# Delta-rule recurrence with loads behind the update, and gates at the head of TensorE's step

## The reference, cut to what matters

```
def step(S, inp):
    qt, kt, vt, at, bt = inp
    err = jnp.einsum('bhij,bhj->bhi', S, kt) - vt
    S = at[..., None] * S - bt[..., None, None] * (err[..., None] * kt[:, :, None, :])
    o = jnp.einsum('bhij,bhj->bhi', S, qt)
    return (S, o)
```

## Time and profile before

| | us |
|---|---|
| median of 3 runs | 7999.06 |
| lowest, highest | 7984.93, 7999.54 |
| profiled execution | 7956.72 |
| its span | 7954.9 |
| VectorE busy | 5439.6 (68%) |
| TensorE busy | 5251.1 (66%) |
| GpSimd busy | 3640.6 (46%) |
| ScalarE (ACT) busy | 3251.7 (41%) |
| mean granted TensorE clock | 0.748 of 2.4 GHz |

### The profile page before, as it was taken

The page is one execution under the profiler, slowest core; times in us unless marked ns, Lnnn a source line. Parts: engine busy times, 40 slices in busy tenths (PEclk is TensorE's granted clock), DMA queues, the critical chain, the costliest instruction groups (busy, mean ns, idle before and its releaser), DMA issues. The chain is left out here.

```text
span 7954.9 us, 175685 instructions
## 1 busy us (share of the span) xinstructions
PE 5251.1 (66%) x58695; PEld 3467.7 (44%) x58695; DVE 5439.6 (68%) x16005; ACT 3251.7 (41%) x6914; POOL 3640.6 (46%) x4232
## 2 busy tenths in 40 slices
PE   5665656656565565655656653577777777777787
PEld 4444444444444444444444443333333333433333
DVE  5777777777877778777777775566656565565655
ACT  4434344343343434434434342244444444344444
POOL 3666676666766667666666666111111111111110
PEclk7766667666676666767767676688888888888888
DMA  4556565565655656556565564111111111121111
GB/s 108 131 133 141 123 144 131 133 141 123 144 128 135 140 122 147 128 134 142 125 143 129 133 144 110 51 44 40 43 40 43 40 40 47 51 50 41 43 40 33
DMA packets 1172906, 786.91 MB, mean 99 GB/s; under 512 B 1039923, under 2 KB 1091795, under 8 KB 1157844
## 3 DMA queue, kind: packets, MB, share of 16 engines
q1 hardware_dynamic: 864468, 583.96, 31.6%
q10 hardware_dynamic: 307712, 193.48, 10.1%
HBM read 473.80 MB, written 303.50 MB: 98 GB/s over the span
## 5 line engine op out<-in xcount | busy, mean ns | idle before, releaser
L588 PE MATMUL p_bank<-xnT,wqkv 128*128 128x128 f32 x4096 | 708.4, 348 | 571.7 <-ACT st L652 571.7
L461 POOL TENSOR_TENSOR qp<-qp,pt 128x512 f32<-128x512 f32 (+7 forms) x1024 | 965.8, 943 | 85.4 <-issue 5.2
L493 PE MATMUL d_bank<-xd,kt 32*64 32x128 f32 x7936 | 411.8, 363 | 881.4 <-issue 399.2
L456 POOL TENSOR_TENSOR qp<-qp,ab 128x512 f32<-128x512 f32 (+7 forms) x1024 | 906.9, 886 | 75.3
L588 PEld LDWEIGHTS p_bank<-xnT,wqkv 128*128 128x128 f32 x4096 | 669.8, 258 | 598.9 <-issue 598.9
L810 DVE SCALAR_TENSOR_TENSOR p_bank<-y,conv_w,p_bank 128x128 f32<-128x128 f32 x3072 | 828.5, 349 | 93.4 <-ACT p_bank L639 77.3
L1682 DVE TENSOR_REDUCE nmax<-w_bank 128x1 f32<-128x512 f32 x1024 | 638.2, 684 | 325.4 <-PE w_bank L1308 315.6
L1263 POOL TENSOR_TENSOR ot<-ot,ln_w 128x1024 f32<-128x1024 f32 x64 | 150.6, 2353 | 1424.2 <-ACT ot L1538 1424.2
L458 POOL TENSOR_TENSOR pt<-qp,vb 128x512 f32<-128x512 f32 (+7 forms) x1024 | 792.6, 774 | 9.3 <-DVE vb L887 9.3
L828 DVE TENSOR_TENSOR st<-d_bank,st 128x512 f32<-128x512 f32 x496 | 320.2, 687 | 674.0 <-PE d_bank L493 661.5
L493 PEld LDWEIGHTS d_bank<-xd,kt 32*64 32x64 f32 x7936 | 327.0, 182 | 940.3 <-issue 934.4
(11 more groups left out here) (219 smaller groups left out, 11569.3 us busy)
## 6 DMA issues: line engine op xcount, KB each, us to landing
decay_or_prod<-decay_dram SPq DMA_DIRECT2D x124, 1024.0 KB, 15.5
prod_dram<-decay_or_prod ACTq DMA_DIRECT2D x64, 1280.0 KB, 7.7
kp<-prod_dram SPq DMA_DIRECT2D x64, 640.0 KB, 6.9
qp<-prod_dram SPq DMA_DIRECT2D x64, 640.0 KB, 9.7
a_dram<-at ACTq DMA_DIRECT2D x64, 512.0 KB
ab<-a_dram SPq DMA_DIRECT2D x64, 512.0 KB, 5.9
v_dram<-vt ACTq DMA_DIRECT2D x64, 512.0 KB
vb<-v_dram SPq DMA_DIRECT2D x64, 512.0 KB, 3.9
```

The lines of the kernel that those rows point to most:

```text
L456: link(nc.gpsimd.tensor_tensor(q, q, ab[:, g, r:r + 1, :].to_broadcast([128, w, DV]), ALU.mult), 1)
L461: link(nc.gpsimd.tensor_tensor(q, q, pt2[:, 0:w], ALU.add))
L493: last[e] = nc.tensor.matmul(d_bank[e][64 * par:64 * par + 64, 128 * k:128 * k + 128], kt[32 * q:32 * q + 32, g, DK * h:DK * h + DK], xd[3 ...
L588: mm = nc.tensor.matmul(bank[:, 128 * i:128 * i + 128], wqkv[:, k, 128 * m:128 * m + 128], xnT[:, g, k, :], start=k == 0, stop=k == 1)
```

## The change

Four things are done.

1. SyncE issues the two spread loads of the decays for step s - 1 in slot s, behind the eight `xd` loads and ahead of `o_dram`, where before it issued them at the end of slot s - 1.
2. The norm belongs to s + 3 in place of s + 2. On VectorE it now lies between the two halves, and between its links lie tap groups 9 to 17, the decay and the state additions; the first nine tap groups stand together ahead of the first half. The load of x for s + 4 is issued behind `xk`, and waits there for the norm of s + 3. The loop starts one step earlier.
3. TensorE transposes `xn` and makes the two gate products of s + 2 between projections 2, 3 and 4 at the head of its step; only the betas stay behind projection 5.
4. ACT evicts the transposes behind projection 2 and ahead of the first silu. Its sigmoids stay where they were.

```diff
+DECAY_AFTER_TAPS, STATE_AFTER_TAPS = 11, (11, 14, 15, 17)
...
-        FIRST, LOOP, LAST = -3, (4, STEPS - 5), STEPS
+        FIRST, LOOP, LAST = -4, (4, STEPS - 5), STEPS
...
+                if updates(lo - 1, hi - 1):
+
+                    sp.wait_ge(*dma_of(dec_wr, n, g, -1))
+                    held(sp, sp_passed)
+                    for par in range(2):
+                        rows = decay_dram[o][par:par + 1].to_broadcast([64, GB * HP, DV])
+                        sp.dma_start(db[64 * par:64 * par + 64], rows).then_inc(db_in[o], 16)
...
-                if valid(lo + 3, hi + 3):
-                    if due(s + 3):
-                        sp.wait_ge(xn_ready, s + 3)
-                    held(sp, sp_passed)
-                    load_x(n + 1 + g, o)
...
+                if valid(lo + 4, hi + 4):
+                    if due(s + 4):
+                        sp.wait_ge(xn_ready, s + 4)
+                    held(sp, sp_passed)
+                    load_x(n + 2, g)
...
-                if updates(lo, hi):
-
-                    sp.wait_ge(*dma_of(dec_wr, n, g, 0))
-                    held(sp, sp_passed)
-                    for par in range(2):
-                        rows = decay_dram[g][par:par + 1].to_broadcast([64, GB * HP, DV])
-                        sp.dma_start(db[64 * par:64 * par + 64], rows).then_inc(db_in[g], 16)
...
                 if front:
-                    for j in range(2, CONV_BANKS - 1):
-                        project(s + 1, 1 - g, j)
+                    project(s + 1, 1 - g, 2)
+                if ahead:
+                    transposed(s + 2, g)
+                    gate(s + 2, g, 0)
+                if front:
+                    project(s + 1, 1 - g, 3)
+                if ahead:
+                    gate(s + 2, g, 1)
+                if front:
+                    project(s + 1, 1 - g, 4)
                 if state:
                     update(*before, (0,))
                 if front:
-                    project(s + 1, 1 - g, CONV_BANKS - 1)
+                    project(s + 1, 1 - g, 5)
                 if ahead:
-                    gates(s + 2, g)
                     betas(s + 2, g)
...
                 if front:
-                    for j in range(2, CONV_BANKS):
-                        evict(s + 1, 1 - g, j)
-                        if j < CONV_BANKS - 1:
-                            silu(s + 1, 1 - g, j - 2)
+                    evict(s + 1, 1 - g, 2)
                 if ahead:
                     transposed(s + 2, g)
+                if front:
+                    for j in range(3, CONV_BANKS):
+                        silu(s + 1, 1 - g, j - 3)
+                        evict(s + 1, 1 - g, j)
+                if ahead:
                     gates(s + 2, n + 1, g)
                     betas(s + 2, n + 1, g)
...
+                    for k in range(TAP_GROUPS // 2):
+                        conv(s + 1, k)
+                if now:
+                    half(s, n, g, 0)
+                groups = iter(range(TAP_GROUPS // 2, TAP_GROUPS))
+
+                def between_halves():
+                    k = next(groups, None)
                     if k is not None and front:
                         conv(s + 1, k)
+                    if k == DECAY_AFTER_TAPS and update:
+                        decay(s - 1, n - 1 + g, 1 - g)
+                    if k in STATE_AFTER_TAPS and update:
+                        for u in range(2):
+                            state(s - 1, 1 - g, 2 * STATE_AFTER_TAPS.index(k) + u)
+
+                if valid(lo + 3, hi + 3):
+                    norm(s + 3, n + 1 + g, 1 - g, between_halves)
                 for _ in range(TAP_GROUPS):
-                    more_taps()
+                    between_halves()
                 if now:
                     half(s, n, g, 1)
```

More of the change, by code:

```diff
@@ L522, in products, with transposed @@
                     mm.then_inc(p_filled, 1)
-            def gates(s, g):
+            def transposed(s, g):
                 bank = use(front1_use(s), 0)
@@ L530, in gates, with gate @@
                 pe.wait_ge(f_freed, front1_use(s) + 1)
[L531 to L535, removed]
+            def gate(s, g, j):
+                bank = use(front1_use(s), 1 + j)
+                for k in range(2):
+                    nc.tensor.matmul(bank[:], xnT[:, g, k, :], wa[:, k, 512 * j:512 * j + 512], start=k == 0, stop=False)
+                nc.tensor.matmul(bank[:], ones[:], ba[:, 512 * j:512 * j + 512], start=False, stop=True).then_inc(f_filled, 1)
             def betas(s, g):
@@ L916, in slot @@
                 if front:
[L917 to L922, removed]
+                    for k in range(TAP_GROUPS // 2):
[5 more added lines that the diff above has]
+                    k = next(groups, None)
                     if k is not None and front:
                         conv(s + 1, k)
[L926 to L937, removed]
-                for _ in range(TAP_GROUPS):
-                    more_taps()
-                if now:
-                    half(s, n, g, 0)
-                taps(9, 10, 11)
-                if update:
-                    decay(s - 1, n - 1 + g, 1 - g)
-                states(0)
-                taps(12, 13, 14)
-                states(1)
-                taps(15)
-                states(2)
-                taps(16, 17)
-                states(3)
+                    if k == DECAY_AFTER_TAPS and update:
[5 more added lines that the diff above has]
+                    norm(s + 3, n + 1 + g, 1 - g, between_halves)
+                for _ in range(TAP_GROUPS):
+                    between_halves()
                 if now:
```

## The result

The median is 7860.4 us (7853.0 to 7875.7, 4 runs) against 7999.3 for the kernel before (7984.9 to 8006.4): a ratio of 0.9839, 95% interval 0.9820 to 0.9857. The gain is 139 us, or 1.6%; the forecast was 308 us.

What follows compares the result with a forecast made beforehand. A chain of waits, no full engine, was taken to set the step: 36.6 + 1.1 + 33.3 = 71.0 us against 76.06, over about 61 steps 308 us less, so 7691; range 7570 to 7870, chance 0.69.

Steps and rivals of the forecast that it cites:

- what bounds the step: No engine is full; a chain of waits sets the 76.06 us step, with late gates ahead of the cross matmuls.
- The wait for the decays: VectorE's decay multiplication, with the decay loads behind `xd`, would wait 0 to 1 us, covered by its wait for update 1.
- the upper end: Slow bound of the forecast: cross at v+38.7 (v: issue of `vb`, the step's start), the full 2.4 us for `a_dram`; 7870.
- the signs of being wrong: `e_dram` issued past v+31; VectorE idle over 3 us before decays; cross waiting for gates' sigmoid; first update beyond v+25.
- 36.6 + 1.1 + 33.3: Step sum, 71.0 us: step start to cross matmuls, price of the `a_dram` write, cross to next step start.
- the term of `a_dram`: The 512 KB gate write moves into the full DMA stretch: 1.1 us a step taken, bounds nothing and 2.4.
- the arm from cross to v: From the cross matmuls to the next issue of `vb`: 33.3 us, read from the last step with an update.
- v to cross without the clash: Issue of `vb` to cross matmuls, without the price of the `a_dram` write: 36.6 us, bounds 33.3 and 38.7.
- the early `xd`: `xd` ahead of the decays takes some 9 us off update 0, but update 0 is no longer late: counted nothing.
- The rivals: More gain, 7510, chance 0.09; nothing, stall moves from `xd` to `e`, 7985 to 8010, 0.08; slower, late `e_dram`, 8130, 0.14.

Runs made afterwards that it cites:

- gates_write_late: The changed kernel with ACT's write of `a_dram` (512 KB) issued behind the last silu: 7644.9 us, ratio 0.9608.
- next_loads_first: The changed kernel with `o_dram`, `ab` and `nb` issued ahead of `xd` and the decays: 7769.9 us, ratio 0.9748.
- warm_cross: The changed kernel with eight matmuls of 512 columns, results unused, on TensorE ahead of the wait for `xe`: 7759.9 us, ratio 0.9733.

## Why the prediction was right or wrong

**Right: what bounds the step.** The gates were on the chain to cross and are off it; cross waits for `e_dram`, at half clock; `xd` is issued in under 4 us; VectorE still waits for the updates behind the decays (578.9 us in all); the norm's move costs nothing (ratio 0.9996); SyncE's wait for xn (191.5 us in all) hides ahead of the wait for `v_dram`. The wait for the decays was forecast at 0 to 1 us and is 2.8 us a step, just short of the 3 that I had named as a sign of being wrong.

The median lies inside the forecast's 7570 to 7870, but with some luck. A step of 74.6 us lies outside its 69 to 74, and the upper end was added up too low: 38.7 + 2.4 + 33.3 is 74.4 us, which by the same sum is 7898. One of the signs of being wrong came, the issue of `e_dram` past v+31 (v+31.5 in the mean).

**Wrong: the size, by 3.6 us a step, in three terms.** The sum was 36.6 + 1.1 + 33.3. By the medians the error is smaller, 169 us or 2.7 a step, for the reason given with the result; the terms below are read from the traces.

First, the term of `a_dram`. I took 1.1 us, with 2.4 as the upper bound, its bytes at the rate of the full stretch. Measured: 3.45 us a step when it is moved away (2.9 by the ratios), 2.45 for a second copy (2.7). It doesn't only share the engines with `e`. Where it falls on the load of `nb`, that takes 5 us and more to issue where it takes 1.8 with the late write, and `e_dram` stands behind it in the queue. The Trainium skill (DMA: Bandwidth & Descriptors, "Issuing engines are not separate DMA queues") had the right sign here, and its rule agrees with these runs; the figure of 2.4 us that I drew from it and from the rate was still too low. This term was wrong by 2.4 us (1.8 by the ratios), two thirds of the error either way.

Second, the arm from cross to v. I took 33.3 us from the last step with an update, which has nothing of a later step behind it. The kernel before took 34.5 in the mean, the changed one takes 35.3. Here I had chosen the nearest picture and not asked what else was missing in it; 2.0 us. The cross at half clock doesn't explain them, since that step had it too (3.48 us; 3.65 now). In the means of the changed kernel, set beside that step, 1.0 of the 2.0 us arise between the last update and the last of the scores matmuls; what those wait for, the trace doesn't name. The Trainium skill (TensorE: Matmul & The Clock Gate, "HAM oscillation") has each burst of matmuls behind a wait for a DMA start at half clock again, and for cross the trace agrees (granted clock 0.54 in the mean, 0.98 before the change). That all updates behind it would then be slow was my reading of it, and they aren't (1.10 and 1.98 in one step).

Third, v to cross without the clash: 36.6 was taken, and gates_write_late has 35.7, 0.9 better. But it is right for the wrong reason. I wrote that the same transfers lie ahead of `e` and so nothing changes. The bytes are the same, the time in which they are moved is not: the decays used to fill the stretch in which SyncE waits for `upd_dram`, and 0.3 MB less have been moved by v+28. `e_dram` leaves at v+28.8 in gates_write_late and at v+27.1 with the decays at their old place as well. Cross has only 0.3 us of that, as the betas hold it there. The rest of the 1.2 to 1.9 us a step that the decays' place costs lies behind cross, and why is not shown. I had put the early `xd` at nothing gained, which was right beside the head gates, and its price at nothing, which was not: with the write that it brings forward it is 5.3 us a step.

**The rivals.** The stall did move from `xd` to `ab`, as the rivals had it, and `e_dram` leaves 3.6 us later (v+31.5), short of the v+32.8 from which it would have been slower. The issue alone doesn't decide, though: in next_loads_first it is 11 us earlier and cross 1.2. And of the 3.6 us by which `e_dram` leaves later, 2.7 go with the late write of `a_dram`, though `ab` still takes 10.6 us to issue there (means); so the stall of `ab` is not what made it late, which the rivals had not seen.

**What stays open.** Why a 512 KB write costs more than its bytes at the rate of the stretch, if it does (2.9 us by the ratios, 2.5 to 3.4, against 2.4); why it holds up the small load of `nb` most; what lengthens the arm behind cross; why 256-byte rows together with a decay load run at so low a rate; and what part of warm_cross's gain is not the clock's.

## What to carry to other kernels

A transfer that is moved out of a queue's way may leave a hole where it was: compare what the DMA engines move in the stretch that it leaves, not only the sum of the bytes. Here that was a small part of the price, and half filling the hole gave nothing. When one part of a change makes an engine earlier, look at what that engine writes next, and into which transfers it then falls; and look at many steps for it, since a single one can show a rare case. And try the parts of a change alone: here one of them gave 5.4%, and the other took two thirds of it back.

## What the runs showed of the hardware

A DMA issue on SyncE's queue is held up by what is queued ahead: the same `ab` load (2048 rows of 256 bytes) took 2.09 us to issue and 9.95 behind the decays, and eight `xd` loads 11.34 us behind them and 3.76 ahead. A 256 KB write that lands in 2.2 us took 10 behind 2 MB in its queue (next_loads_first). A 512 KB write on ACT's queue cost 2.5 to 3.5 us a step, through transfers of SyncE's queue: in 24 of 61 steps a small load (`nb`) took 5 to 7.5 us to issue, where it takes 1.8 with the write out of the way. Large rows and rows of 256 bytes together moved 110 GB/s in one stretch where large ones almost alone moved 202 (131 and 208 in the means over the steps).
